# A four-layer attention model on one core: transfers of 29 and 125 rows of layer 2 in two pieces each

## The chip, the core and the metric

The kernel is one program on one core of a Trainium2 chip. The metric is device time in microseconds (us). The profiled core has five compute engines (TensorE, in the views PE, with PEld for its weight loads; VectorE, DVE; ScalarE, ACT; GpSimd, POOL; SyncE, SP, which here only issues transfers) and 16 DMA engines that move data between HBM (DRAM) and the on-chip memories. A DMA goes onto a queue in the order in which SP issues it and counts up a semaphore by 16 when it has landed; whoever needs the data waits for the count.

## What is computed

Four layers of attention and feed-forward run over x (16 batches of 56 tokens, 128 features) with a context of 16 x 1500 x 128. Everything is float32 in layer 2. The change is in layer 2's attention: 16 heads of 64 features, keys and values from the normed context, and one learned null key and value in front.

```python
def _L2_xattn_ref(x, context, mask, ln1_s, ln1_b, lnc_s, lnc_b, Wq, Wkv, null_kv, Wo, lno_s, lno_b):
    ...
    xn = _ln(x, ln1_s, ln1_b)
    cn = _ln(context, lnc_s, lnc_b)
    q = xn @ Wq
    kv = cn @ Wkv
    k, v = jnp.split(kv, 2, axis=-1)
    ...
    k = jnp.concatenate((nk, k), axis=2)
    v = jnp.concatenate((nv, v), axis=2)
    sim = jnp.einsum('bhid,bhjd->bhij', q * scale, k)
    ...
    sim = jnp.where(mfull, sim, max_neg)
    attn = jax.nn.softmax(sim, axis=-1)
    out = jnp.einsum('bhij,bhjd->bhid', attn, v)
    out = out.transpose(0, 2, 1, 3).reshape(b, n, h * d)
    out = out @ Wo
    return _ln(out, lno_s, lno_b)
```

## The kernel before

`attention_16_wide_heads` folds the weights (Wq with Wk, Wv with Wo), so that scores are taken against the normed context itself and the weighted sums are taken of it as well. For each of the 16 batches the 16 heads x 56 queries are 896 rows of queries: seven tiles of 128 (`RT = 7`), 112 tiles in all. The 1500 keys of a batch are laid out as `CH = 125` rows of `NCH = 12` keys each, 128 features (512 bytes) a key, so that one row of the context in DRAM is 6144 bytes. The rows are cut into `WINDOWS = 4` windows: three of `BW = 32` rows, and a last one of `LAST_KEYS = 29` rows. A window gives 12 blocks of 32 keys, and a batch has 48 blocks.

The context goes two ways. For the scores it comes turned (features on partitions, `L2keys`, two slots) and GpSimd norms it there (`normalise_keys`: subtract the means, line 1719, multiply by the scales, line 1721), with means and scales spread over partitions by `load_moments` (L2mean_spread and L2wqk, from L_moments in DRAM). For the weighted sums it comes with keys on partitions: `load_raw` (line 1547) brings 125 rows into L2raw, GpSimd norms them in place (`normalise_values`, lines 1727 and 1729), `store_values` (line 1551) writes the result to DRAM as L_normal_context, and `load_values(b, w)` (line 1560) reads one window of it back four times, into the four quadrants of 32 partitions of L2values. In other words the context is normed once, and the quadrant layout is made by the readback. L2raw is one buffer, so `load_raw(b)` waits until the store before it has landed.

TensorE goes through n = 1, 2, ...: `scores(n)` (line 1636, four matmuls in the program, eight records in the trace) and eight tiles later `weigh(n - 8)` (line 1653), step g of batch b, which takes blocks 7g to 7g + 6 (the last step six) in four quadrants: 56 or 48 records. Step g waits for the windows that its blocks lie in; the sixth step (blocks 35 to 41) is the first to need the last window. Behind `scores`, VectorE takes the maximum (line 1826), ScalarE exponentiates (1764) and scales (1769), VectorE transposes (1836); `take_heads` on ScalarE (1774) empties a batch's sums. ScalarE makes the mask of batch b + 1 (line 1782) between two tiles of batch b, from L2mask, which SP loads.

SP's order is written out by hand: first the fill, down to `load_values(0, w)`, and then for each batch b: keys of b + 1; windows 2 and 3 of b - 1; raw of b + 2; window 0 of b; moments of b + 2; window 1 of b; store of b + 2; mask of b + 2. SP waits before many of these: window w of batch b is loaded when `weigh` is past the last step of batch b - 1 that reads it (`pv_done`), keys when the slot's scores are done, the store when GpSimd has normed (`v_ready`). `TT` is 112.

Of the kernel before, what the change touches and what calls it, by code (L numbers as in the profile page):

```python
# [13 lines left out]
P = 128  # L14
B, Q, S2 = 16, 56, 1500
TOK = B * Q
TT = 2 * Q
NTT = TOK // TT
CH, NCH = 125, 12
# [10 lines left out]
class Vectors:  # L30
# [6 lines left out]
    at = {}  # L37
# [1358 lines left out]
WINDOWS = 4  # L1396
BW = 32
BLOCKS = WINDOWS * NCH
LAST_KEYS = CH - (WINDOWS - 1) * BW
# [3 lines left out]
WORK_COLUMNS = 2 * SM_COLUMNS + CELLS  # L1403
LAG = RT + 1
KEY_COLUMNS = S2 + 3


class WideAhead:
# [61 lines left out]
def attention_16_wide_heads(nc, k, src, ahead):  # L1470
# [8 lines left out]
    with ExitStack() as ctx:  # L1479
# [48 lines left out]
        def block_cells(a, b, block):  # L1528
# [3 lines left out]
                return of.rearrange("p (g r t n) -> p g r t n", g=RT, r=RT, t=RT)[:, g, r]  # L1532
            return of.rearrange("p (t r g n) -> p t r g n", t=RT, r=RT, g=RT)[:, :, r, g]

        def step_blocks(g):
            return range(RT * g, min(RT * g + RT, BLOCKS))

# [2 lines left out]
        @block.sync  # L1540
        def _(sp):
            def load_raw(b):
                if b:
                    sp.wait_ge(s.v_stored, 16 * b)
                else:
                    sp.wait_ge(s.v_zeroed, 2)
                sp.dma_start(RAW[:, :, 0:P - 1], src["ctx"][b][:, :, 0:P - 1]).then_inc(s.raw_loaded, 16)

            def store_values(b):
                sp.wait_ge(s.v_ready, b + 1)  # L1550
                sp.dma_start(normal[b], RAW[:]).then_inc(s.v_stored, 16)

            def load_values(b, w):
                sp.wait_ge(s.v_stored, 16 * (b + 1))
                if b:
                    last_step = (NCH * w + NCH - 1) // RT
                    sp.wait_ge(s.pv_done, RT * (b - 1) + last_step + 1)
                n = BW if w < WINDOWS - 1 else LAST_KEYS
                for a in range(4):
                    sp.dma_start(V[a * BW:a * BW + n, w * NCH:(w + 1) * NCH, :], normal[b][w * BW:w * BW + n]  # L1560
                                 ).then_inc(values_loaded[w], 16)

            def load_mask(b):
                if b:
                    sp.wait_ge(s.mask_ready, 2 * b)
                sp.dma_start(MR[:], src["mask_full"][b].partition_broadcast(P)).then_inc(s.mask_loaded, 16)

            def load_keys(b):
                if b < 2:
                    sp.wait_ge(s.slot_ready, 2 * b + 2)  # L1570
                else:
                    sp.wait_ge(s.scores_filled, RT * (b - 1))
                for rows in (slice(0, TT), slice(TT, P - 1)):
                    sp.dma_start(KT[rows, b % 2, 0:S2], src["ctxT"][b][rows]).then_inc(keys_loaded[b % 2], 16)

            def load_moments(b):
                if b == 1:
                    sp.wait_ge(s.q_filled, 2 * H)
                if b:
                    sp.wait_ge(s.keys_scaled, b)  # L1580
                for x, to in enumerate((MEAN[:], scale_of(b))):
                    sp.dma_start(to, scratch[x, b].rearrange("c n -> (c n)").partition_broadcast(P)).then_inc(s.spread_loaded, 16)

            load_mask(0)
            load_keys(0)
            sp.wait_ge(s.moments_ready, 1)
            sp.dma_start(scratch.rearrange("k (h b) c n -> (b c) (k h) n", h=2), MOMENTS).then_inc(s.moments_stored, 16)
            load_raw(0)
            sp.wait_ge(s.moments_stored, 16)
            load_moments(0)  # L1590
            for a in range(4):
                at = a * BW + LAST_KEYS
                sp.dma_start(V[at:at + 1, BLOCKS - 1, :], k.ident[P - 1:P, :]).then_inc(s.null_rows, 16)
            load_keys(1)
            store_values(0)
            load_raw(1)
            load_moments(1)
            store_values(1)
            load_raw(2)
            load_mask(1)  # L1600
            for w in range(WINDOWS):
                load_values(0, w)
            load_moments(2)
            store_values(2)
            load_mask(2)
            for b in range(1, B + 1):
                ahead_of = b + 2 < B
                if b + 1 < B:
                    load_keys(b + 1)
                if b >= 2:  # L1610
                    load_values(b - 1, 2)
                    load_values(b - 1, 3)
                if ahead_of:
                    load_raw(b + 2)
                if b < B:
                    load_values(b, 0)
                if ahead_of:
                    load_moments(b + 2)
                if b < B:
                    load_values(b, 1)  # L1620
                if ahead_of:
                    store_values(b + 2)
                    load_mask(b + 2)

        @block.tensor
        def _(pe):
# [12 lines left out]
            def weigh(step):  # L1639
                b, g = divmod(step, RT)  # L1640
                if g == 0:
                    pe.wait_ge(s.turned, RT * b + RT)
                    if b:
                        pe.wait_ge(s.heads_ready, 4 * b)
                    else:
                        pe.wait_ge(s.max_done, LAG)
                        pe.wait_ge(s.null_rows, 64)
                blocks = step_blocks(g)
                for w in range(blocks[0] // NCH, blocks[-1] // NCH + 1):
                    pe.wait_ge(values_loaded[w], 64 * (b + 1))  # L1650
                for n in blocks:
                    for a in range(4):
                        last = nc.tensor.matmul(PS[:, 4 + a, 0:RT * BW], V[a * BW:(a + 1) * BW, n, :], block_cells(a, b, n),  # L1653
                                                start=n == 0, stop=n == BLOCKS - 1, tile_position=(a * BW, 0))
                last.then_inc(s.pv_done, 1)
# [55 lines left out]
        @block.gpsimd  # L1711
        def _(pool):
            def normalise_keys(b):
                pool.wait_ge(keys_loaded[b % 2], 32 * (b // 2 + 1))
                pool.wait_ge(s.spread_loaded, 32 * (b + 1))
                if b == 0:
                    pool.wait_ge(s.slot_ready, 4)
                keys = KT[0:P - 1, b % 2, 0:S2]
                nc.gpsimd.tensor_tensor(keys, keys, MEAN[0:P - 1], ALU.subtract).then_inc(s.keys_moved, 1)  # L1719
                pool.wait_ge(s.keys_moved, b + 1)  # L1720
                nc.gpsimd.tensor_tensor(keys, keys, scale_of(b)[0:P - 1], ALU.mult).then_inc(s.keys_scaled, 1)

            def normalise_values(b):
                pool.wait_ge(s.raw_loaded, 16 * (b + 1))
                x = RAW[:, :, 0:P - 1]
                spread = lambda of: of.unsqueeze(2).to_broadcast([CH, NCH, P - 1])
                nc.gpsimd.tensor_tensor(x, x, spread(k.ctx_mv[:, b, :, 0]), ALU.subtract).then_inc(s.v_centred, 1)  # L1727
                pool.wait_ge(s.v_centred, b + 1)
                nc.gpsimd.tensor_tensor(x, x, spread(rs[:, b, :]), ALU.mult).then_inc(s.v_ready, 1)

            for u in range(2):
                nc.gpsimd.memset(KT[:, u, :], 0.0).then_inc(s.slot_ready, 1)
                pool.wait_ge(s.slot_ready, 2 * u + 1)
                nc.gpsimd.tensor_copy(KT[:, u, S2:S2 + 1], k.ident[:, P - 1:P]).then_inc(s.slot_ready, 1)
                if u == 0:
                    ln_pool(pool, k, s)
                    pool.wait_ge(s.ln_rstd, 2)
            nc.gpsimd.memset(RAW[:, :, P - 1:P], 0.0).then_inc(s.v_zeroed, 1)
            nc.gpsimd.memset(V[:, (WINDOWS - 1) * NCH:, :], 0.0).then_inc(s.v_zeroed, 1)
            nc.gpsimd.memset(BIG[:], FLT_MAX).then_inc(s.constants, 1)  # L1740
            for u in range(2):
                nc.gpsimd.memset(MA[:, u, WINDOWS - 1, :, LAST_KEYS:BW], FLT_MAX).then_inc(s.margins, 1)
            for u in range(2):
                pool.wait_ge(s.margins, u + 1)
                nc.gpsimd.memset(MA[:, u, WINDOWS - 1, NCH - 1, LAST_KEYS:LAST_KEYS + 1], 0.0).then_inc(s.margins, 1)
            pool.wait_ge(s.margins, 4)
            normalise_keys(0)
            normalise_values(0)
            normalise_keys(1)
            normalise_values(1)  # L1750
            normalise_values(2)
            for b in range(1, B - 1):
                normalise_keys(b + 1)
                if b + 2 < B:
                    normalise_values(b + 2)
            ln_pool(pool, k, s2)
# [942 lines left out]
```

## Time and profile before

| | us |
|---|---|
| median of 3 runs | 2424.81 |
| lowest, highest | 2419.15, 2427.26 |
| the profiled execution | 2429.18 |
| its span in the trace | 2427.4 |
| layer 2's attention within it, about | 850 to 1880 |
| PE busy over the span | 2000.4 (82%) |
| DVE, ACT, POOL busy | 1416.2, 1256.3, 833.6 |
| granted clock of TensorE, mean | 0.899 |

The profile page gives busy time by engine, by line and in slices; the trace behind it can be asked for one engine's instructions in order of time, for the waits of an engine with what ended them, and for stretches: how long each engine was busy in a stretch, the mean clock that TensorE was granted (1.00 is 2.4 GHz, 0.50 is 1.2 GHz), the mean busy share of the 16 DMA engines and what they moved. A row of SPq is the issue of a transfer, and its time is how long the issue held SP's queue, not how long the transfer took. Merged rows (x8) run from the first start to the last end.

### The profile page before, as it was taken

How to read it: one execution, taken by the hardware profiler on the slowest of the kernel's cores; microseconds unless marked ns; L12 is line 12 of the kernel's file. 1: busy time of each engine (PE TensorE's matmuls, PEld its weight loads, DVE VectorE, ACT ScalarE, POOL GpSimd, SP SyncE). 2: the span in 40 equal slices, each digit the busy share in tenths (PEclk: the TensorE clock that was granted, in tenths of full speed). 3: DMA queues.
4: the chain of work that ended last, by engine and by line, in shares of the span. 5: the costliest groups of instructions: out<-in, count | busy, mean ns of one | idle time of the engine just before them, and what ended most of it. 6: DMA issues, size and time to landing. Idle time of an engine off the chain costs nothing. (4 is left out here: it accounts for less than half of the span.)

```text
span 2427.4 us, 51483 instructions
## 1 busy us (share of the span) xinstructions
PE 2000.4 (82%) x21121; PEld 1419.8 (58%) x21121; DVE 1416.2 (58%) x2762; ACT 1256.3 (52%) x2169; POOL 833.6 (34%) x376
## 2 busy tenths in 40 slices
PE   6999999669988993877776666666687779999997
PEld 3777777458874462555554444444465436777774
DVE  5777777789855443544444444444440667777784
ACT  5787877337652233544444444444440247777773
POOL 6656562157756532221212121212100044444410
PEclk8999999679998986988888888888888889999997
DMA  6454542325403043544344444344420144444430
GB/s 164 137 152 137 150 139 78 87 72 142 141 18 80 26 120 107 135 119 119 120 121 120 122 121 119 119 119 119 132 69 11 31 120 139 138 130 137 134 93 9
DMA packets 130282, 263.70 MB, mean 109 GB/s; under 512 B 69456, under 2 KB 77696, under 8 KB 129792
## 3 DMA queue, kind: packets, MB, share of 16 engines
q1 hardware_dynamic: 130048, 260.40, 37.6%
q8 instruction: 168, 2.75, 0.5%
q14 instruction: 66, 0.54, 0.1%
HBM read 167.57 MB, written 12.94 MB: 74 GB/s over the span
## 5 line engine op out<-in xcount | busy, mean ns | idle before, releaser
L1653 PE MATMUL L2ps<-L2work,L2values 32*128 32x224 f32 x6144 | 354.9, 382 | 241.4 <-DMA L2values<-L_normal_context 235.6
L1653 PEld LDWEIGHTS L2ps<-L2work,L2values 32*128 32x128 f32 x6144 | 318.1, 203 | 302.0 <-issue 295.2
L1836 DVE STREAM_TRANSPOSE L2work<-L2work 128x1568 f32<-128x1568 f32 x112 | 202.9, 1811 | 369.3 <-PE L2ps L1653 367.7
L1769 ACT ACTIVATE L2work<-L2work,L2rinv 128x1536 f32<-128x1536 f32 x112 | 176.8, 1579 | 370.9 <-DVE L2rinv L1841 370.9
L1636 PE MATMUL L2ps<-L2keys,L2qz 128*128 128x384 f32 x896 | 329.7, 510 | 42.5 <-DVE L2negmax L1826 35.1
L1826 DVE CUSTOM_DVE_ANT_0 L2work<-L2ps,L2maskadd,L2big 128x1536 f32<-128x1536 f32 x112 | 203.6, 1818 | 105.0 <-PE L2ps L1636 105.0
L1636 PEld LDWEIGHTS L2ps<-L2keys,L2qz 128*128 128x128 f32 x896 | 161.8, 190 | 173.9 <-issue 39.9
L1764 ACT ACTIVATE L2work<-L2work,L2negmax 128x1536 f32<-128x1536 f32 x112 | 176.2, 1573 | 119.9 <-DVE L2negmax L1826 119.8
L654 ACT ACTIVATE L3probsT<-L3ps 128x448 f32<-128x448 f32 x384 | 196.1, 547 | 71.0 <-PE L3ps L511 66.4
L654 ACT ACTIVATE L0probsT<-L0ps 128x448 f32<-128x448 f32 x384 | 198.2, 552 | 47.5 <-PE L0ps L511 46.4
L798 DVE TENSOR_REDUCE L0partmax<-L0ps 112x1 f32<-112x1000 f32 x128 | 153.4, 1199 | 58.7 <-PE L0ps L484 56.8
L1727 POOL TENSOR_TENSOR L2raw<-L2raw,ctx_mv 125x1524 f32<-125x1524 f32 x16 | 43.9, 2743 | 417.8 <-DMA L2raw<-in_ctx 417.8
L798 DVE TENSOR_REDUCE L3partmax<-L3ps 112x1 f32<-112x1000 f32 x128 | 153.4, 1198 | 57.6 <-PE L3ps L484 55.4
L511 PEld LDWEIGHTS L0ps<-L0query_stack,L0key_stack 99*128 99x128 bf16 x1536 | 110.6, 99 | 57.4 <-issue 13.6
L1719 POOL TENSOR_TENSOR L2keys<-L2keys,L2mean_spread 127x1500 f32<-127x1500 f32 x16 | 49.8, 3110 | 270.9 <-DMA L2keys<-in_ctxT 230.2
L511 PEld LDWEIGHTS L3ps<-L3query_stack,L3key_stack 98*128 98x128 bf16 x1536 | 110.5, 99 | 54.8 <-issue 13.8
L511 PE MATMUL L0ps<-L0query_stack,L0key_stack 99*128 99x112 bf16 x1536 | 134.0, 214 | 0.7 <-ACT L0probsT L654 0.6
L511 PE MATMUL L3ps<-L3query_stack,L3key_stack 98*128 98x112 bf16 x1536 | 133.3, 214 | 0.0
L605 POOL TENSOR_TENSOR L3keys<-L3keys,L3key_parts 128x1500 f32<-128x1500 f32 x16 | 48.6, 3037 | 193.3 <-ACT L3key_parts L701 193.3
L793 DVE TENSOR_REDUCE L0partmax<-L0ps 112x1 f32<-112x500 f32 x128 | 86.3, 674 | 33.1 <-PE L0ps L476 33.1
L793 DVE TENSOR_REDUCE L3partmax<-L3ps 112x1 f32<-112x500 f32 x128 | 86.2, 673 | 30.8 <-PE L3ps L476 30.8
L498 PE MATMUL L3ps<-L3probsT,L3values 128*32 128x112 f32 x3072 | 99.8, 263 | 0.0
(478 smaller groups left out, 3877.1 us busy)
## 6 DMA issues: line engine op xcount, KB each, us to landing
L2values<-L_normal_context SPq DMA_DIRECT2D x192, 192.0 KB
L0key_stack<-L0key_parts SPq DMA_DIRECT2D x192, 187.5 KB
L3key_stack<-L3key_parts SPq DMA_DIRECT2D x192, 187.5 KB
L0ctxT<-in_ctxT SPq DMA_DIRECT2D x16, 750.0 KB, 4.4
L1rawT<-in_ctxT SPq DMA_DIRECT2D x16, 750.0 KB, 6.5
L2mean_spread<-L_moments SPq DMA_DIRECT2D x16, 750.0 KB, 7.2
L_normal_context<-L2raw SPq DMA_DIRECT2D x16, 750.0 KB
L3ctxT<-in_ctxT SPq DMA_DIRECT2D x16, 750.0 KB, 4.4
```

Of the source, the lines that this page charges most:

```text
L498: last = nc.tensor.matmul(PS[32 * g:32 * g + 32, 3, u * TT:(u + 1) * TT], V[:, b % 2, value_columns(c, 4 * u + g)], PT[:, u, c, g, :], sta ...
L511: last = nc.tensor.matmul(PS[:, bank, c * TT:(c + 1) * TT], KS[:, h % 4, tau, key_columns(4 * j + c)], QS[:, h % 4, tau, :], start=True, s ...
L654: ins = nc.scalar.activation(PT[:, h % 2, 4 * j:4 * j + 4, tau, :], PS[:, bank, 0:HALF].rearrange("p (c n) -> p c n", c=4), ACT.Exp)
L793: nc.vector.tensor_reduce(PM[:, h % 2, tau, 0:1], PS[0:TT, 0, 0:500], AX.X, ALU.max).then_inc(s.m0_done, 1)
L798: nc.vector.tensor_reduce(PM[:, h % 2, tau, 1:2], PS[0:TT, 1:3, 0:500], AX.XY, ALU.max).then_inc(s.m12_done, 1)
L1636: last = nc.tensor.matmul(PS[:, score_bank(m) + w, 0:NCH * BW], tile_rows(m), key_window(b, w), start=True, stop=True)
L1653: last = nc.tensor.matmul(PS[:, 4 + a, 0:RT * BW], V[a * BW:(a + 1) * BW, n, :], block_cells(a, b, n), start=n == 0, stop=n == BLOCKS - 1, ...
L1719: nc.gpsimd.tensor_tensor(keys, keys, MEAN[0:P - 1], ALU.subtract).then_inc(s.keys_moved, 1)
L1764: nc.scalar.activation(SM[:, m % 2, 0:NPR], SM[:, m % 2, 0:NPR], ACT.Exp, bias=nmax[:, m % 4:m % 4 + 1], scale=-1.0, accum_out=ssum[:, m % ...
L1769: nc.scalar.mul(SM[:, m % 2, 0:NPR], SM[:, m % 2, 0:NPR], rinv[:, m % 4:m % 4 + 1]).then_inc(s.scaled, 1)
L1826: nc.vector.tensor_tensor_reduce(SM[:, m % 2, 0:NPR].rearrange("p (w n) -> p w n", w=WINDOWS), PS[:, bank:bank + 4, 0:NCH * BW], MA[:, m / ...
L1836: nc.vector.transpose(turned_cells(b, t), SM[:, m % 2].rearrange("p (g r n) -> p g r n", g=RT, n=BW)).then_inc(s.turned, 1)
```

## The change

`load_raw` and `store_values` send their 125 rows as two transfers, of 112 and of 13 rows. `load_values` sends the last window's 29 rows, for each of the four quadrants, as 16 and 13 rows; the other windows stay transfers of 32 rows. The same bytes go to the same places. The counts that are waited for follow: 32 for each batch of raw and of the store in place of 16, and 128 in place of 64 for the last window.

```diff
--- before.py
+++ after.py
@@ -1403,6 +1403,7 @@
 WORK_COLUMNS = 2 * SM_COLUMNS + CELLS
 LAG = RT + 1
 KEY_COLUMNS = S2 + 3
+WHOLE, SHORT = (slice(0, BW),), (slice(0, BW // 2), slice(BW // 2, LAST_KEYS))
 
 
 class WideAhead:
@@ -1532,6 +1533,9 @@
                 return of.rearrange("p (g r t n) -> p g r t n", g=RT, r=RT, t=RT)[:, g, r]
             return of.rearrange("p (t r g n) -> p t r g n", t=RT, r=RT, g=RT)[:, :, r, g]
 
+        window_rows = lambda w: WHOLE if w < WINDOWS - 1 else SHORT
+        values_count = lambda b, w: 64 * len(window_rows(w)) * (b + 1)
+
         def step_blocks(g):
             return range(RT * g, min(RT * g + RT, BLOCKS))
 
@@ -1541,24 +1545,26 @@
         def _(sp):
             def load_raw(b):
                 if b:
-                    sp.wait_ge(s.v_stored, 16 * b)
+                    sp.wait_ge(s.v_stored, 32 * b)
                 else:
                     sp.wait_ge(s.v_zeroed, 2)
-                sp.dma_start(RAW[:, :, 0:P - 1], src["ctx"][b][:, :, 0:P - 1]).then_inc(s.raw_loaded, 16)
+                for rows in (slice(0, TT), slice(TT, CH)):
+                    sp.dma_start(RAW[rows, :, 0:P - 1], src["ctx"][b][rows, :, 0:P - 1]).then_inc(s.raw_loaded, 16)
 
             def store_values(b):
                 sp.wait_ge(s.v_ready, b + 1)
-                sp.dma_start(normal[b], RAW[:]).then_inc(s.v_stored, 16)
+                for rows in (slice(0, TT), slice(TT, CH)):
+                    sp.dma_start(normal[b][rows], RAW[rows]).then_inc(s.v_stored, 16)
 
             def load_values(b, w):
-                sp.wait_ge(s.v_stored, 16 * (b + 1))
+                sp.wait_ge(s.v_stored, 32 * (b + 1))
                 if b:
                     last_step = (NCH * w + NCH - 1) // RT
                     sp.wait_ge(s.pv_done, RT * (b - 1) + last_step + 1)
-                n = BW if w < WINDOWS - 1 else LAST_KEYS
                 for a in range(4):
-                    sp.dma_start(V[a * BW:a * BW + n, w * NCH:(w + 1) * NCH, :], normal[b][w * BW:w * BW + n]
-                                 ).then_inc(values_loaded[w], 16)
+                    for rows in window_rows(w):
+                        to, of = (slice(at + rows.start, at + rows.stop) for at in (a * BW, w * BW))
+                        sp.dma_start(V[to, w * NCH:(w + 1) * NCH, :], normal[b][of]).then_inc(values_loaded[w], 16)
 
             def load_mask(b):
                 if b:
@@ -1647,7 +1653,7 @@
                         pe.wait_ge(s.null_rows, 64)
                 blocks = step_blocks(g)
                 for w in range(blocks[0] // NCH, blocks[-1] // NCH + 1):
-                    pe.wait_ge(values_loaded[w], 64 * (b + 1))
+                    pe.wait_ge(values_loaded[w], values_count(b, w))
                 for n in blocks:
                     for a in range(4):
                         last = nc.tensor.matmul(PS[:, 4 + a, 0:RT * BW], V[a * BW:(a + 1) * BW, n, :], block_cells(a, b, n),
@@ -1721,7 +1727,7 @@
                 nc.gpsimd.tensor_tensor(keys, keys, scale_of(b)[0:P - 1], ALU.mult).then_inc(s.keys_scaled, 1)
 
             def normalise_values(b):
-                pool.wait_ge(s.raw_loaded, 16 * (b + 1))
+                pool.wait_ge(s.raw_loaded, 32 * (b + 1))
                 x = RAW[:, :, 0:P - 1]
                 spread = lambda of: of.unsqueeze(2).to_broadcast([CH, NCH, P - 1])
                 nc.gpsimd.tensor_tensor(x, x, spread(k.ctx_mv[:, b, :, 0]), ALU.subtract).then_inc(s.v_centred, 1)
```

Nothing else changes its place; line numbers below line 1406 grow by 1 to 6. SP's part for one batch in the middle of the stage, before:

```order
L1574 DMA L2keys<-in_ctxT 112x1500
L1574 DMA L2keys<-in_ctxT 15x1500
L1560 DMA L2values<-L_normal_context 32x1536 x4
L1560 DMA L2values<-L_normal_context 29x1536 x4
L1547 DMA L2raw<-in_ctx 125x12x127
L1560 DMA L2values<-L_normal_context 32x1536 x4
L1582 DMA L2mean_spread<-L_moments 128x1500
L1582 DMA L2wqk<-L_moments 128x1500
L1560 DMA L2values<-L_normal_context 32x1536 x4
L1551 DMA L_normal_context<-L2raw 125x1536
L1566 DMA L2mask<-in_mask_full 128x1500
```

And the same place in the changed kernel. L2wqk holds the scales from L_moments here; of the last window's eight transfers the first two stand:

```order
L1580 DMA L2keys<-in_ctxT 112x1500
L1580 DMA L2keys<-in_ctxT 15x1500
L1567 DMA L2values<-L_normal_context 32x1536 x4
L1567 DMA L2values<-L_normal_context 16x1536
L1567 DMA L2values<-L_normal_context 13x1536
```

Three more pairs of 16 and 13 rows follow, and then:

```order
L1552 DMA L2raw<-in_ctx 112x12x127
L1552 DMA L2raw<-in_ctx 13x12x127
L1567 DMA L2values<-L_normal_context 32x1536 x4
L1588 DMA L2mean_spread<-L_moments 128x1500
L1588 DMA L2wqk<-L_moments 128x1500
L1567 DMA L2values<-L_normal_context 32x1536 x4
L1557 DMA L_normal_context<-L2raw 112x1536
L1557 DMA L_normal_context<-L2raw 13x1536
```

SP's order is kept: the keys, the two windows, raw, window 0, moments, window 1, store, and 23 transfers of a batch become 29. The second place is the fill, on SP too: the stores of batches 0 and 1, the loads of raw 1 and 2, and the mask of batch 1. Before:

```order
L1551 DMA L_normal_context<-L2raw 125x1536
L1547 DMA L2raw<-in_ctx 125x12x127
L1582 DMA L2mean_spread<-L_moments 128x1500
L1582 DMA L2wqk<-L_moments 128x1500
L1551 DMA L_normal_context<-L2raw 125x1536
L1547 DMA L2raw<-in_ctx 125x12x127
L1566 DMA L2mask<-in_mask_full 128x1500
```

In the changed kernel:

```order
L1557 DMA L_normal_context<-L2raw 112x1536
L1557 DMA L_normal_context<-L2raw 13x1536
L1552 DMA L2raw<-in_ctx 112x12x127
L1552 DMA L2raw<-in_ctx 13x12x127
L1588 DMA L2mean_spread<-L_moments 128x1500
L1588 DMA L2wqk<-L_moments 128x1500
L1557 DMA L_normal_context<-L2raw 112x1536
L1557 DMA L_normal_context<-L2raw 13x1536
L1552 DMA L2raw<-in_ctx 112x12x127
L1552 DMA L2raw<-in_ctx 13x12x127
L1572 DMA L2mask<-in_mask_full 128x1500
```

Store, raw and the mask of batch 1 stay in this order, with a transfer of 13 rows behind each of 112.

## Rows read from the trace of the kernel before

**Rows 1.** Waits of PE, 960 to 1860: total us, times, longest us.

```profile
PE L2ps L1653 <- DMA L2values<-L_normal_context: 235.6, 28, 18.6
PE L2ps L1636 <- POOL L2keys L1721: 7.2, 1, 7.2
```

**Rows 2.** PE in order of time: start, us, line, operation, tiles, count, idle time before.

```profile
1209.99 2.93 PE L1653 MATMUL L2ps<-L2work,L2values 32*128 32x224 f32 x56
...
1231.51 4.67 PE L1653 MATMUL L2ps<-L2work,L2values 32*128 32x224 f32 x56 [15.75 <-DMA L2values<-L_normal_context]
...
1238.97 2.55 PE L1653 MATMUL L2ps<-L2work,L2values 32*128 32x224 f32 x48
...
1250.99 2.93 PE L1653 MATMUL L2ps<-L2work,L2values 32*128 32x224 f32 x56 [0.91 <-DMA L2values<-L_normal_context]
...
1290.29 4.30 PE L1653 MATMUL L2ps<-L2work,L2values 32*128 32x224 f32 x56 [16.39 <-DMA L2values<-L_normal_context]
...
1526.37 5.61 PE L1653 MATMUL L2ps<-L2work,L2values 32*128 32x224 f32 x56 [16.17 <-DMA L2values<-L_normal_context]
```

**Rows 3.** Stretches: window, length, PE, PEld, DVE, ACT, POOL busy, PEclk, DMA share, GB/s.

```profile
1172.00:1231.00 59.00, 41.59 (x440) 29.67 (x440) 25.78 (x28) 25.11 (x27) 12.22 (x4) 0.85 0.40 121
1194.00:1212.00 18.00, 18.00 (x218) 12.92 (x214) 11.05 (x12) 9.48 (x10) 6.74 (x2) 1.00 0.27 85
1222.00:1230.00 8.00, 0.00 (x0) 0.00 (x0) 0.00 (x0) 0.00 (x0) 0.00 (x0) 0.50 0.06 26
1212.00:1221.00 9.00, 3.77 (x28) 2.00 (x22) 3.68 (x4) 6.40 (x7) 0.00 (x0) 0.84 0.31 93
1240.00:1247.00 7.00, 7.00 (x98) 5.18 (x92) 4.68 (x6) 4.85 (x8) 5.48 (x2) 1.00 1.00 309
546.50:551.00 4.50, 4.29 (x29) 3.20 (x28) 3.97 (x27) 4.44 (x13) 3.37 (x3) 1.00 0.90 224
```

**Rows 4.** SP's queue in order of time, 1246 to 1306, its longest entries.

```profile
1250.58 12.75 SPq L1560 DMA_DIRECT2D L2values<-L_normal_context  x8
1263.37 7.20 SPq L1547 DMA_DIRECT2D L2raw<-in_ctx  x1
...
1270.68 25.41 SPq L1560 DMA_DIRECT2D L2values<-L_normal_context  x4
...
1297.13 2.39 SPq L1560 DMA_DIRECT2D L2values<-L_normal_context  x4
```

**Rows 5.** PE in order of time: the wait for keys, and the last steps.

```profile
1001.37 5.32 PE L1636 MATMUL L2ps<-L2keys,L2qz 128*128 128x384 f32 x8 [7.21 <-POOL L2keys L1721]
...
1807.50 6.88 PE L1653 MATMUL L2ps<-L2work,L2values 32*128 32x224 f32 x104 [2.29 <-DMA L2values<-L_normal_context]
...
1844.50 7.64 PE L1653 MATMUL L2ps<-L2work,L2values 32*128 32x224 f32 x104 [11.68 <-DMA L2values<-L_normal_context]
```

**Rows 6.** The fill, 862 to 949, all engines in order of time.

```profile
862.58 26.23 PE L1682 MATMUL L2ps<-xnT,L2wqk 128*128 128x448 f32 x64 [0.84 <-DVE xnT L163]
...
911.64 2.85 POOL L1719 TENSOR_TENSOR L2keys<-L2keys,L2mean_spread 127x1500 f32<-127x1500 f32 x1 [23.37 <-DMA L2wqk<-L_moments]
...
922.94 0.28 SPq L1551 DMA_DIRECT2D L_normal_context<-L2raw  x1
930.42 0.82 SPq L1547 DMA_DIRECT2D L2raw<-in_ctx  x1
931.29 6.08 SPq L1566 DMA_DIRECT2D L2mask<-in_mask_full  x1
...
942.88 1.26 ACT L1782 ACTIVATE L2maskadd<-L2mask,L2big 128x1152 f32<-128x1152 uint8 x1 [31.04 <-DMA L2mask<-in_mask_full]
...
948.22 10.29 PE L1636 MATMUL L2ps<-L2keys,L2qz 128*128 128x384 f32 x24 [33.21 <-DVE L2negmax L1826]
```

**Rows 7.** The page's part on DMA issues: count, KB each, median us to landing.

```profile
L0ctxT<-in_ctxT SPq DMA_DIRECT2D x16, 750.0 KB, 4.4
...
L2mean_spread<-L_moments SPq DMA_DIRECT2D x16, 750.0 KB, 7.2
```

## What the change should do, before it was run

> **What bounds the kernel now.** I read the waits of PE in the stretch of layer 2's attention first, then PE's order in time over two batches, then what the DMA engines did while PE stood still, then SP's order in time. The first view says where the time is: of the 900 us that it covers, PE stood 235.6 us for L2values, in 28 waits, and 7.2 us for keys [rows 1]. The second shows the pattern: one long wait a batch (13.4 to 18.6 us, 13 of them), always before the sixth of the seven steps of `weigh`, the first that needs the last window (29 rows), and a wait under 1 us at the second step [rows 2]. After each long wait the next step takes 4.30 to 5.61 us where an undisturbed one takes 2.93 [rows 2]: the granted clock is 0.50 while PE stands and 1.00 while it works [rows 3], so that is the lower of the two levels, 1.2 against 2.4 GHz. Between waits PE is busy 18.00 of 18.00 us, with VectorE at 11.05, ScalarE at 9.48 and GpSimd at 6.74 [rows 3]: nothing but the transfers stands in PE's way.
>
> The third view says why the transfers are late. While PE waits, DMA share is 0.06 and 26 GB/s: one engine of 16 [rows 3]. The four transfers of 29 rows are 4 x 174 KB = 0.71 MB, and 0.71 MB at 26 GB/s is 27.4 us. With the 125-row load of L2raw issued behind them the share is 0.31 [rows 3], five of 16: four with the load's parts, the fifth still with the 29 rows. So I read that 29 rows go through one engine and 125 rows through five, of which that one is a member. Its time in one batch is then: 29-row transfers 27.4; its fifth of L2raw 9 (the others take 1212 to 1221); its fifth of the 125-row store, 154 KB at 26 GB/s, 5.9; and a sixteenth of the rest. A batch moves 59 us x 121 GB/s = 7.1 MB [rows 3]; less 0.71, 0.76 and 0.77 that leaves 4.9 MB, which at 309 GB/s, all engines busy [rows 3], takes 15.9 us. Sum 58.2 us, against a batch of 1290.29 - 1231.51 = 58.8 us [rows 2]. The bound is one DMA engine, not PE. SP shows the same: four of its entries hold the queue 12.75 + 7.20 + 25.41 + 2.39 = 47.8 us a batch, though the same kind of four transfers takes 2.39 once and 25.41 another time [rows 4].
>
> **The change part by part.** (1) Each 29-row transfer becomes 16 + 13 rows, each 125-row one 112 + 13. Bytes stay. The trace has no 13-row transfer by itself; the nearest stretch is layer 1's attention, which loads its context as 112 + 13 rows, where the share is 0.90 at 224 GB/s, mixed with other loads [rows 3]. Best end: all spreads, 7.1 MB at 309 GB/s is 23 us of engine time a batch. Worst end: every 13-row piece stays on one engine. Then that one has 52 of 116 rows of the last window (12.3 us), 13 rows of raw (13/125 x 5 x 9 = 4.7), 13 of the store (80 KB, 3.1), its sixteenth of the 112- and 16-row pieces (1.4 MB at 309 GB/s, 4.5) and the 15.9 of before: 40.5 us. I take the spread end, by the 0.90 of layer 1, and keep the other for the range.
>
> The Trainium skill, DMA: Bandwidth & Descriptors, "Why a DMA increments its semaphore by 16 and not by 1", says that a transfer issued from SP uses the largest number up to 16 that divides its row count: 1 for 29, 5 for 125, 16 for 112 and for 16, 13 for 13. The trace agrees for 29 and 125 (shares 0.06 and 0.31), and shows neither 13 nor 16 alone. By that rule the sum is that of the spread end.
>
> (2) What PE needs for a batch when it never waits: 58.8 - 16.39 - 0.91 - (4.67 - 2.93) = 39.8 us [rows 2]. The 23 us of transfers fit, and they have time to land: the last window's are released at the end of step seven of the batch before and needed before step six, five and a half of seven steps or 31 us on; their eight issues cost some 0.5 us each (2.39 for four [rows 4]) and 0.71 MB at 309 GB/s is 2.3 us, under 10 us with what lies in front. So all of the 235.6 us goes, and what is late next is nothing: max, exp, scale and turn kept up with PE at exactly this rate in the 18 us above. Term: 235.6.
>
> (3) PE's slow step after each of the 13 long waits, 4.30 to 5.61 (lowest and highest shown, mean of the 13 5.00) [rows 2], goes too: 13 x (5.00 - 2.93) = 26.9.
>
> (4) One wait for keys, 7.2 us [rows 1], with eight records of `scores` in 5.32 behind it [rows 5], where 2.9 is the undisturbed figure: those keys were loaded late by the same held queue. Term: 9.6.
>
> (5) The end: two groups of 104 take 6.88 and 7.64 [rows 5] where 2.93 + 2.55 less overlap is 5.4 [rows 2]. Term: 3.7.
>
> (6) The fill. PE stands 33.21 us before 948.22; the chain behind it is mask(1), which ScalarE awaits 31.04 us, until 942.88 [rows 6]. Back from it: mask(1) is issued behind raw(2) and held 6.08; raw(2) waits 7.5 us for store(1) to land; store(1) follows GpSimd's keys(1) and values(1), 11.3 us from 911.64; and keys(1) waited for moments(1) [rows 6]. Afterwards: moments(1) can go out at 888.8, when PE's 26.23 us group ends; with 0.3 us for issue and a landing of 7.2 [rows 7] keys(1) starts at about 896.5; store(1) 907.8; landing 4.4, the row of a 750 KB transfer without a queue [rows 7], raw(2) at 912.2; mask(1) lands 12.5 - 6.1 = 6.4 later, about 919. That is 24 us sooner. The bounds: 31.0, when mask(1) is never awaited, and 10 if raw and store gain nothing but the 6.08 and half of the store's 7.5. The 3 MB of values for batch 0 go out from 913 and need 10 us, before the first `weigh` at about 937. Term: 24.
>
> (7) Added: per batch four issues for values, one for raw, one for the store, 6 x 0.5 = 3 us of SP. SP then has some 13 us of work in 39.8, so it costs nothing; if SP were still held all the time it would be 16 x 3 = 48. The counts waited for grow with the number of transfers, so nobody waits for less or more data. SP's waits for `pv_done` and `v_ready` still stand in front of the transfers queued behind them, each over 20 us ahead of its reader.
>
> Sum: 235.6 + 26.9 + 9.6 + 3.7 + 24 = 299.8. Against the profiled execution, 2429.2 (span 2427.4 and 1.8 around it), that is 2129.4. This execution lies 4.4 above the median 2424.8, so for the median I forecast **2125**.
>
> **Rivals.** (A) The 13-row pieces do not spread. One engine has 40.5 us a batch against PE's 39.8, so short waits stay, 1 to 2 us with a slow step behind some: 15 x 2.5 = 38, 2163. For it: no row shows such a piece alone. Against: 0.90 in layer 1.
> (B) The change doesn't do what it says: two pieces take together what one took, and one engine keeps them. The batch stays at 58.8 and the time at 2425. Against it: the share of 0.06 leaves 15 engines with nothing to do. The Trainium skill, DMA: Bandwidth & Descriptors, "Rules for kernel authors", says just this: don't split a transfer into disjoint partition halves, they serialize on the same 16 engines. It supposes that the whole used all 16; the row with 0.06 says otherwise here.
> (C) Slower: SP's hold is a price of each transfer and not of a full engine behind it. Four entries hold SP 47.8 us for 17 transfers, 2.8 each; six more add 17 us, and 47.8 + 17 = 64.8 exceeds the 58.8 of a batch by 6: 2425 + 15 x 6 = 2515. It decides from 11/6 = 1.8 us for each added transfer. Against it: four of the same take 2.39 us together [rows 4].
> (D) The fill gains only 10, or a wait of about 1 us a batch remains at the second step: 14 to 15 more, 2140. That is within the forecast's own spread.
>
> **How the numbers follow.** Forecast with (D), 2112 to 2145: 0.80. (A), 2145 to 2175: 0.11. (B), 2405 to 2435: 0.04. (C): 0.03. The rest, 0.02, is another bound between 2175 and 2400. The low end is the sum with 31 in the fill and 5 more for the last steps and the clock; the high end takes in (A) up to 2168. This range holds about 0.9, since the price of (A) is no clearer than this. A measurement of this kernel can tell about 0.3%, 7 us, from no change: faster 0.94, same 0.03, slower 0.03.
>
> **What would show it.** In the profile of the changed kernel: no PE wait of more than 3 us for L2values; batches 39.8 us apart; the DMA share never at 0.06 for more than 3 us inside this stage, and about 175 GB/s on average; SP's entries for raw under 2 us; the clock at 1.00 over the stage; mask(1) landed near 919. Wrong would be: a share of 0.06 behind the 13-row pieces (A), unchanged waits (B), SP entries of over 1.8 us for each small piece (C).

## The result, and the profile after it

The changed kernel takes 2123.72 us (median of 4 runs, 2121.64 to 2124.81) against 2426.03 us of the kernel before: the ratio is 0.8754, 95% interval 0.8729 to 0.8778. The forecast was 2125, with a range of 2112 to 2168. Run again it took 2123.34 us, ratio 0.8761 (0.8749 to 0.8773).

The waits of TensorE from 900 to 1570 in the changed kernel (total us, times, longest), which answer to [rows 1]:

```profile
PE L2ps L1642 <- DVE L2negmax L1832: 12.3, 5, 10.0
PE L2ps L1659 <- DVE L2work L1842: 5.8, 2, 3.2
PE L2ps L1712 <- ACT L2qz L1780: 1.2, 1, 1.2
```

The 28 waits for L2values and the one for keys are gone. What is left lies in the fill (12.3) and at the two ends of the batches' chain (5.8). In the middle of the stage, TensorE in order of time, answering to [rows 2]:

```profile
1131.36 2.55 PE L1659 MATMUL L2ps<-L2work,L2values 32*128 32x224 f32 x48
...
1170.94 2.55 PE L1659 MATMUL L2ps<-L2work,L2values 32*128 32x224 f32 x48
```

These are the last steps of two batches in a row, 39.58 us apart. In the kernel before, the forecast took 58.8 from one pair of batches; the last steps from 1006.62 to 1474.53 are 58.5 apart in the mean of eight. The stretch from 1000 to 1450, with the columns of [rows 3] (window, length, busy times, granted clock, DMA share, GB/s):

```profile
1000.00:1450.00 450.00, 450.00 (x5017) 315.11 (x5019) 293.27 (x320) 285.83 (x307) 129.12 (x44) 1.00 0.72 180
```

TensorE is busy 450.00 of 450.00 us at a clock of 1.00, the DMA engines are busy 0.72 of the time instead of 0.40, and the same bytes go at 180 GB/s instead of 121. SP's queue over one batch, answering to [rows 4]:

```profile
1137.27 1.68 SPq L1552 DMA_DIRECT2D L2raw<-in_ctx  x2
1145.44 2.39 SPq L1567 DMA_DIRECT2D L2values<-L_normal_context  x4
...
1156.88 2.52 SPq L1567 DMA_DIRECT2D L2values<-L_normal_context  x4
...
1170.10 6.71 SPq L1567 DMA_DIRECT2D L2values<-L_normal_context  x12
```

Two transfers of raw hold SP 1.68 us where one held it 7.20, and window 0 takes 2.39 where it took 25.41. The fill, answering to [rows 6], and the end of the stage, answering to [rows 5]:

```profile
919.08 1.26 ACT L1788 ACTIVATE L2maskadd<-L2mask,L2big 128x1152 f32<-128x1152 uint8 x1 [7.79 <-DMA L2mask<-in_mask_full]
...
924.41 6.97 PE L1642 MATMUL L2ps<-L2keys,L2qz 128*128 128x384 f32 x16 [9.96 <-DVE L2negmax L1832]
...
937.24 4.62 PE L1659 MATMUL L2ps<-L2work,L2values 32*128 32x224 f32 x56 [2.54 <-DVE L2work L1842]
...
1529.65 18.44 PE L1659 MATMUL L2ps<-L2work,L2values 32*128 32x224 f32 x384 [3.23 <-DVE L2work L1842]
```

The mask of batch 1 lands at 919.08 (before 942.88), TensorE resumes at 924.41 (before 948.22), and the last sums end at 1548.09 (1529.65 + 18.44) where they ended at 1852.14 (1844.50 + 7.64): 304.0 us of the 304.4 by which the spans differ.

### The profile page after: what moved, and what is told of

Same layout as the page of the kernel before. It is cut to its first block and busy times, and to the rows that moved or that the text cites. A ratio compares the mean times of both kernels' runs of the same rounds, so it can differ in the third digit from the quotient of the medians.

```text
span 2123.0 us, 51579 instructions
## 1 busy us (share of the span) xinstructions
PE 1962.9 (92%) x21121; PEld 1386.9 (65%) x21121; DVE 1415.5 (67%) x2762; ACT 1255.4 (59%) x2169; POOL 833.1 (39%) x376
## 5 line engine op out<-in xcount | busy, mean ns | idle before, releaser
L1642 PE MATMUL L2ps<-L2keys,L2qz 128*128 128x384 f32 x896 | 327.0, 507 | 12.3 <-DVE L2negmax L1832 12.3
L1659 PEld LDWEIGHTS L2ps<-L2work,L2values 32*128 32x128 f32 x6144 | 285.4, 186 | 64.5 <-issue 57.8
L1659 PE MATMUL L2ps<-L2work,L2values 32*128 32x224 f32 x6144 | 321.9, 356 | 5.8 <-DVE L2work L1842 5.8
L511 PEld LDWEIGHTS L0ps<-L0query_stack,L0key_stack 99*128 99x128 bf16 x1536 | 110.6, 99 | 58.5 <-issue 13.5
L498 PE MATMUL L3ps<-L3probsT,L3values 128*32 128x112 f32 x3072 | 99.8, 263 | 0.0
L498 PE MATMUL L0ps<-L0probsT,L0values 128*32 128x112 f32 x3072 | 99.7, 263 | 0.0
```

Source lines behind the costliest of these rows:

```text
L498: last = nc.tensor.matmul(PS[32 * g:32 * g + 32, 3, u * TT:(u + 1) * TT], V[:, b % 2, value_columns(c, 4 * u + g)], PT[:, u, c, g, :], sta ...
L511: last = nc.tensor.matmul(PS[:, bank, c * TT:(c + 1) * TT], KS[:, h % 4, tau, key_columns(4 * j + c)], QS[:, h % 4, tau, :], start=True, s ...
L1642: last = nc.tensor.matmul(PS[:, score_bank(m) + w, 0:NCH * BW], tile_rows(m), key_window(b, w), start=True, stop=True)
```

## The experiments

The forecast rested on one sum: how long one DMA engine is busy with a batch, against how long TensorE is. The experiments take the change apart, and then vary the row count alone, with the number of transfers kept.

**Only the last window in two pieces.** Raw and store are whole again.

```diff
-                for rows in (slice(0, TT), slice(TT, CH)):
+                for rows in (slice(0, CH),):
                     sp.dma_start(RAW[rows, :, 0:P - 1], ...
...
-                for rows in (slice(0, TT), slice(TT, CH)):
+                for rows in (slice(0, CH),):
                     sp.dma_start(normal[b][rows], RAW[rows]) ...
```

The counts that are waited for are 16 a batch again too.

> Only the last window's 29 rows go as 16 + 13; raw and store are 125 rows in one transfer again. Theory (one DMA engine's time per batch sets the batch before, PE's 39.8 us after): that engine has 9 (its fifth of raw) + 5.9 (store) + about 1 (last window) + 15.9 (its sixteenth of the rest) = 32 us, under 39.8, so PE never waits for values in the middle and batches stay 39.5 to 39.8 us apart; only the fill loses its 24 us: 2124 + 24 = 2148 (2140 to 2160). Rival (raw, the widest transfer in descriptors, is what held SP 7 to 25 us a batch): with raw whole SP stays held and most of the waits come back, over 2250.

Measured: 2145.68 us, ratio 0.8856 (0.8834 to 0.8878), which is 22.0 more than the changed kernel. TensorE's waits over the stage, and its restart in the fill:

```profile
PE L2ps L1642 <- DVE L2negmax L1832: 30.9, 1, 30.9
PE L2ps L1659 <- DVE L2work L1842: 5.1, 2, 3.2
```

```profile
945.26 11.02 PE L1642 MATMUL L2ps<-L2keys,L2qz 128*128 128x384 f32 x24 [30.92 <-DVE L2negmax L1832]
```

No wait for values is left, which rules out the rival, the batches are 39.5 to 39.6 us apart, and the whole loss is the fill: TensorE restarts at 945.26 and not at 924.41, 20.9 us later, and the spans of the two traces differ by 20.9 (2143.9 and 2123.0). So, with 16 + 13 rows in the last window, its split makes the middle and that of raw and store the fill.

**Only raw and store in two pieces.** The last window is one transfer of 29 rows.

```diff
-WHOLE, SHORT = (slice(0, BW),), (slice(0, BW // 2), slice(BW // 2, LAST_KEYS))
+WHOLE, SHORT = (slice(0, BW),), (slice(0, LAST_KEYS),)
```

> Only raw and store are split into 112 + 13; the last window is 29 rows in one transfer, four times. Theory: one engine has 27.4 (29 rows, 0.71 MB at 26 GB/s) + 6.4 MB over all engines at 309 GB/s = 20.7, together 48.1 us a batch: PE waits about 8 us before the sixth step, batches 48 us apart, 2124 + 15 x 8.3 = 2248 (2220 to 2275), the fill as in the changed kernel (mask of batch 1 at about 919). Rival (raw held SP): about 2124 to 2140, without long waits.

Measured: 2307.26 us, ratio 0.9525 (0.9505 to 0.9546), some 59 us slower than expected and outside the range. Its SP queue and one stretch in which nothing else was left to move:

```profile
1197.25 24.46 SPq L1552 DMA_DIRECT2D L2raw<-in_ctx  x2
```

```profile
1152.00:1168.00 16.00, 12.28 (x131) 8.20 (x129) 9.23 (x11) 11.02 (x10) 0.00 (x0) 0.98 0.07 27
```

For 16 us the DMA share is 0.07 at 27 GB/s, one engine of 16, and the two issues of raw, 112 and 13 rows here, hold SP for 24.46 us in the next batch (23.03 in this one). The mechanism is the forecast's (raw did not hold SP by itself: the rival's 2124 to 2140 is out), but the batches are 51.4 to 53.6 us apart, not 48.

**The same number of transfers, other row counts: 23 + 6, 28 + 1, 12 + 17.** All else as in the changed kernel.

```diff
-WHOLE, SHORT = (slice(0, BW),), (slice(0, BW // 2), slice(BW // 2, LAST_KEYS))
+WHOLE, SHORT = (slice(0, BW),), (slice(0, 23), slice(23, LAST_KEYS))
```

and in its place `(slice(0, 28), slice(28, LAST_KEYS))` and `(slice(0, 12), slice(12, LAST_KEYS))`.

> As the changed kernel, but the last window goes as 23 + 6 rows: the same number of transfers and bytes, another row count. Theory (a row count without a divisor up to 16 sits on one engine): 4 x 23 rows = 0.565 MB at 26 GB/s = 21.7 us, and 6.5 MB over all engines = 21.1, and under 1 for the 6 rows: 43.5 us a batch against 39.8, so 2124 + 15 x 3.7 = 2180 (2150 to 2205), waits of 3 to 5 us before the sixth step. Rival (what helps is the smaller transfer, or two in flight at once): 2124 to 2130 as the changed kernel.

> As the changed kernel, but the last window goes as 28 + 1 rows. Theory (28 rows spread over 14 engines, and four single rows cost one engine 1 us): 2124 (2118 to 2130), no waits for values. Rival (only row counts that are a multiple of 16 spread, 13 rows too few to matter): 28 rows on one engine, 26.5 + 20.7 = 47 us a batch, 2124 + 15 x 7.4 = 2235.

> As the changed kernel, but the last window goes as 12 + 17 rows. Theory: 17 rows sit on one engine, 4 x 17 rows = 0.418 MB at 26 GB/s = 16.1 us, with 6.7 MB over all engines 21.6: 37.7 us a batch, just under PE's 39.8. So 2124 (2118 to 2140) although a transfer without a divisor is there: it costs only when its engine's sum passes PE's. Rival (any transfer on one engine is late for its reader, whatever the sum): waits of some us a batch, 2170 and more.

Measured: 23 + 6 takes 2240.2 us (ratio 0.9246, 0.922 to 0.9271), 28 + 1 takes 2123.1 (0.8767, 0.8749 to 0.8785), 12 + 17 takes 2176.8 (0.8966, 0.895 to 0.8982). One stretch of the kernel with 23 rows:

```profile
1188.00:1196.00 8.00, 8.00 (x75) 5.36 (x72) 5.54 (x6) 4.21 (x6) 0.00 (x0) 1.00 0.07 28
```

and one of that with 17:

```profile
1202.00:1211.00 9.00, 9.00 (x105) 6.32 (x108) 6.10 (x7) 4.82 (x4) 0.00 (x0) 1.00 0.06 27
```

Both leave one engine at work, as 29 rows did; 28 rows leave no stretch of 6 us or more like it, and no wait. A smaller transfer, or two in flight, is then not what helped: 23 + 6 and 16 + 13 differ by 116 us with the same count and bytes. Nor does a count have to be a multiple of 16: 28 + 1 equals the change. By the rule of the Trainium skill (DMA: Bandwidth & Descriptors, "Why a DMA increments its semaphore by 16 and not by 1"), that the largest divisor up to 16 sets the number of engines, 23 and 17 get one and 28 gets 14. The shares of 0.07 and 0.06 agree with it for 23 and 17; for 28 the absence of waits shows that it is not one engine, and not that it is 14.

But 23 + 6 was expected at 2180 and 12 + 17 at 2124, so here too the size was wrong, by 60 and 53 us, as by 59 in the run before. Three misses of one sign and size pointed to the term that all three share.

**The term that failed.** In all three the part of a batch that is spread over 16 engines had been taken at 309 GB/s, 23 us. The changed kernel shows it directly, as the mean of its 16 engines: a share of 0.73 over 40 us is 29.2 us. (The long stretch, 0.72 over a batch of 39.6, gives 28.5; the sums below use 29.2, as the forecasts of the next runs do, and would be 0.4 to 0.7 us lower with 28.5.) With 29.2 for 7.1 MB the sums are 53.7, 48.6 and 43.6 us, and the batches were 52.1, 47.5 and 43.4 apart (means between 1000 and 1450). Three more kernels were made to test this sum where it forecasts something of its own.

**Half of the quadrants: 12 + 17, or 29 whole.** Quadrants 0 and 1 differ, 2 and 3 keep 16 + 13.

```diff
-        window_rows = lambda w: WHOLE if w < WINDOWS - 1 else SHORT
+        window_rows = lambda w, a=0: WHOLE if w < WINDOWS - 1 else OTHER if a < 2 else SHORT
...
-                    for rows in window_rows(w):
+                    for rows in window_rows(w, a):
```

with `OTHER` as 12 + 17 rows in the first, and as 29 rows (and the count waited for to match) in the second.

> As the changed kernel, but two of the four quadrants take the last window as 12 + 17 rows, the other two as 16 + 13. Theory, mended after e2, e3 and e5 (the part that all 16 engines share takes each of them 29.2 us a batch, share 0.73 of 40 us in the changed kernel, not 23): 2 x 17 rows = 0.209 MB at 26 GB/s = 8.0 us on one engine, and 29.2 x 6.9/7.1 = 28.3: 36.4 us against 39.6, so no waits and 2124 (2119 to 2131). Rival (each transfer on one engine costs its reader some us, whatever the sum): half of what e5 lost, 53/2: 2150.

> As the changed kernel, but two of the four quadrants take the last window as 29 rows in one transfer. Mended theory: 2 x 29 rows = 0.356 MB = 13.7 us and 29.2 x 6.75/7.1 = 27.7: 41.4 us against 39.6, 15 x 1.8 = 27: 2151 (2135 to 2165). The first theory (23 us shared): 13.7 + 21.8 = 35.5, no waits, 2124. Rival (by whole transfers): half of what e2 lost, 183/2: 2215.

Measured: 2123.76 us for the first (ratio 0.8761, 0.8745 to 0.8777), without waits and with batches 39.5 to 39.6 apart; 2136.99 for the second (0.8819, 0.8805 to 0.8833), with these waits of TensorE:

```profile
PE L2ps L1660 <- DMA L2values<-L_normal_context: 13.6, 9, 2.4
```

So the same 17-row transfers on one engine, which cost 53 us when all four quadrants used them, cost nothing when two do: it is the sum that decides, not the single transfer. The second lies in its range near the lower end, with batches of 39.5 to 43.2 us where 41.4 was worked out.

**Raw and store whole again, with 12 + 17.**

> The last window as 12 + 17 rows, raw and store whole in 125 rows as in the kernel before. Mended theory: the same engine has 16.1 (17 rows), 9 + 5.9 (its fifths of raw and store) and 29.2 x 5.2/7.1 = 21.4: 52 us, and since this way of counting came out 1 to 4 us high in e2 and e3, batches of 49 to 52 us; with the 22 us that e1 lost in the fill: 2124 + 22 + 15 x (9.5 to 12.5) = 2289 to 2334. Rival (raw and store cost nothing in the middle, as e1 seems to say): 2177 + 22 = 2199.

The edit is that of the first experiment with that of 12 + 17. Measured: 2284.83 us, ratio 0.9426 (0.9409 to 0.9443); the waits:

```profile
PE L2ps L1659 <- DMA L2values<-L_normal_context: 104.9, 35, 8.3
```

That is 4 us below the range given and 86 above the rival. The batches are 49.9 us apart, within the 49 to 52 given. Part of why the time still came out lower is the factor of 15: the last batch has no scores beside its sums (18.44 us in the changed kernel), so 14 full periods are paid, and 2146 + 14 x 10.3 is 2290. The 5 us that remain are open. Whole transfers of 125 rows cost 22 us beside 16 + 13, all in the fill, but 108 beside 12 + 17 (2284.8 - 2176.8), where each batch grows by 6.5 us (49.9 - 43.4) and the sum by 8.6. Their share on that engine is free as long as its sum stays under TensorE's 39.6 us, and the greater part of it is paid above.

All kernels in one table, with the mended sum (the engine's own transfers at 26 GB/s, raw's fifth 9 us and the store's 5.9 where whole, and the spread part at 29.2 us for 7.1 MB):

| last window | raw, store | sum for one engine, us | batch measured, us | median, us |
|---|---|---|---|---|
| 29 | whole (before) | 62.5 | 58.5 | 2424.8 |
| 29 | split | 53.7 | 52.1 | 2307.3 |
| 12 + 17 | whole | 52.2 | 49.9 | 2284.8 |
| 23 + 6 | split | 48.6 | 47.5 | 2240.2 |
| 12 + 17 | split | 43.6 | 43.4 | 2176.8 |
| 29 in two quadrants | split | 41.4 | 40.8 | 2137.0 |
| 16 + 13 | whole | 37.8 | 39.6 | 2145.7 |
| 12 + 17 in two quadrants | split | 36.4 | 39.6 | 2123.8 |
| 16 + 13 (the change) | split | 29.2 | 39.6 | 2123.7 |

Below 39.6 TensorE sets the batch, above it the one engine. The sum is a little high where that engine's own part is large, 4.0 us in the kernel before. I did not test why; the spread part was measured with all engines sharing it closely, and it may go faster where they have more room. The stretches bear this out in part only. In the kernel before the share is 0.41 from 1231 to 1290, which is 387 us of all 16 engines together; less 27.4 and five times 14.9 (raw and store) that leaves 17.8 each for the spread part, where the sum took 20.2. With 12 + 17 rows and split raw and store the same working (0.68 over 43.4 us, less 16.1) leaves 28.5, where it took 27.5. From row to row the order is as the sum says; its size holds to 2.3 us or better, and to 4.0 in the kernel before.

**The mask of batch 1 earlier.** The changed kernel's fill still has ScalarE waiting 7.79 us for this mask and TensorE 9.96 behind it.

```diff
+            load_mask(1)
             store_values(1)
             load_raw(2)
-            load_mask(1)
```

> As the changed kernel, but in the fill the mask of batch 1 is loaded ahead of the store of batch 1 and raw of batch 2. Theory: in the changed kernel ScalarE still awaits this mask 7.8 us and PE stands 10.0 us behind it; the mask then lands before 905 and both waits go; the first weighing starts 8 us sooner if the values of batch 0, sent from 913, are there by 929: 2124 - 8 = 2116 (2113 to 2120). Rival: the values of batch 0 are what comes last then, and a wait for them takes up to all of the 8: 2119 to 2124.

Measured: 2115.7 us, ratio 0.8717 (0.8698 to 0.8736). The fill:

```profile
909.88 2.92 PE L1642 MATMUL L2ps<-L2keys,L2qz 128*128 128x384 f32 x8 [2.07 <-DVE L2negmax L1832]
...
922.71 4.62 PE L1659 MATMUL L2ps<-L2work,L2values 32*128 32x224 f32 x56 [2.54 <-DVE L2work L1842]
```

The wait of 9.96 us is 2.07 now, about the time that ScalarE needs to make the mask, and the values are there in time. Since part of the difference in this trace lay ahead of the stage, both kernels were run again on one chip:

> The changed kernel once more, on the same chip as the next run, so that the two can be compared directly: 2124 (2119 to 2128).

> The kernel with the mask of batch 1 loaded early once more. Theory: 8 us less than the changed kernel on the same chip, 2116 (2112 to 2120). Rival: the 8 us between e6 and the changed kernel came from another chip and from a stretch ahead of this stage; then both are equal within 3 us.

2123.34 against 2117.17 us; the ratios to the kernel before are 0.8761 (0.8749 to 0.8773) and 0.8731 (0.8717 to 0.8745), just apart. The gain is 6.2 us, somewhat less than the 8 of theory and 0.3% of the time, near the least that such runs can tell; this is the fastest kernel of the study. The traces show that the gain is not one number. In the second trace of the changed kernel TensorE had worked off the group of 64 matmuls ahead of the scores by 880.75 and not by 888.26, stands 16.15 us for the mask in place of 9.96, and starts the first `weigh` at 935.93, 1.3 us sooner: there the mask hides what an earlier stretch gained or lost. With the mask out of the way it shows: 922.71 and 926.89 for the first `weigh` in the two traces, and times from 2109.48 to 2121.27, where the changed kernel has 2120.41 to 2125.14.

## Why the forecast came out right, and where it was luck

- **What bounds the kernel before.** Right. One DMA engine of 16 was the bound; the row counts 29, 23 and 17 each put a transfer on one.
- **The sum of that engine.** Wrong in one term. The spread part of a batch was taken from a 7 us stretch at 309 GB/s; over a batch it goes at 243 GB/s in the time that the engines are busy (7.1 MB in 29.2 us). No single rate holds at full share: two single microseconds of the changed kernel, both near 1.00, moved 426 and 166 GB/s, the second just as window 1 and the two pieces of the store were issued.

```profile
1271.00:1272.00 1.00, 1.00 (x4) 0.56 (x3) 0.70 (x2) 0.26 (x1) 0.00 (x0) 1.00 1.02 426
1278.00:1279.00 1.00, 1.00 (x17) 0.83 (x20) 0.71 (x1) 1.00 (x1) 0.00 (x0) 1.00 0.93 166
```

The agreement of 58.2 with the batch of 58.8 was partly luck: with the mended term the sum is 62.5, 4 us high. The forecast for the change did not hang on it, since both 23 and 29.2 are under TensorE's time. Every forecast near the threshold did: three experiments missed by 53 to 60 us.
- **TensorE's own 39.8 us.** Right: 39.5 to 39.6. VectorE, ScalarE and GpSimd kept up over 450 us as they had over the 18 that the forecast pointed to.
- **The spread of 13 rows.** Taken at the spread end from the mixed stretch of layer 1. Right, and the changed kernel's trace shows it for the store. The store of batch 0 is issued at 881.10 with all DMA engines at rest, and this is the stretch in which its 112 and its 13 rows move:

```profile
881.75:884.75 3.00, 3.00 (x10) 1.52 (x9) 1.25 (x2) 1.08 (x3) 0.00 (x0) 1.00 0.80 256
```

256 GB/s times 3.00 us is the whole 0.77 MB. If the 13 rows were on one engine, it would need 3.1 us for them and 1.7 for its seven of the 112 rows, at 26 GB/s, and the share could not be 0.80. SP's next issue, raw of batch 1, waits for both pieces and comes 4.2 us after the store's; before it came 7.7 after (888.30 and 895.97).
- **Waits for values, 235.6, and for keys, 7.2.** Right, both are gone. One reading behind them was loose and changed nothing: the wait at the second step was called under 1 us, and in the trace it is 0.36 to 3.03, over 1 in 7 of 13 batches.
- **The slow steps and the clock.** Right: the clock is 1.00 over the stretch of 450 us and no step is slow in it. From the first `weigh` to the end of the last one (961.05 to 1852.14, now 937.24 to 1548.09) the stage shrank by 280.2; the terms for it (235.6 + 26.9 + 9.6 + 3.7) make 275.8. Of the 4.4 us that are missing, up to 2.7 are slow matmuls that the terms left out: TensorE's busy time for scores and sums fell from 329.7 + 354.9 to 327.0 + 321.9, 35.7 us, and the terms hold 33.0 of it. The rest stayed unassigned.
- **The fill.** Right: the first `weigh` starts 23.8 us earlier, the sum said 24, and the mask (919) and the first `weigh` (937) came within 0.3 us of the times given. The steps between did too, within 1.2 us: moments(1) out at 888.29, keys(1) at 895.53, store(1) at 906.84, raw(2) at 911.04. Putting raw and store back cost 22.0. A little luck is in the first step: moments(1) was to go out when TensorE's group of 64 ends, and in the second trace of this kernel that is 880.75, but moments(1) goes out at 886.54, right behind raw(1), which had waited for the store. In the first trace the two conditions are 1.4 us apart (886.84 and 888.26), so the sum did not feel it.
- **SP's six more issues a batch.** Free, as said: SP is not held.
- **The rival of 13 rows on one engine.** Not borne out, but its price of 2163 was too low. The 16- and 112-row pieces are 1.76 MB (0.39 + 0.68 + 0.69), not 1.4. By the mended sum that engine has 12.3 + 4.7 + 3.1 of its own, 7.3 of these pieces and 20.2 of the rest, 47.6 us a batch, and that is about 2240. The range to 2168 did not cover that rival as it claimed to.

## What to carry to other kernels

Before asking how many bytes a transfer has, look at the DMA share while the reader waits: 0.06 of 16 engines at 26 to 28 GB/s over many microseconds means that one of them has the work, and another row count (28 + 1, 16 + 13) can be worth more than any reordering. (A short stretch can mislead: the changed kernel has 0.06 and 23 GB/s from 1282 to 1288, but there all engines are at rest from 1283 to 1287 and busy at either end.) Sum up what the busiest engine does in one period and compare it with the compute engine's time; below that a badly spread transfer is free, above it most of it is paid in each period (here the batch grew by 15.1 us from 43.4 to 58.5 while the sum grew by 18.9). Take the rate of the shared part from a stretch as long as the period, since a short one at its peak flatters it, and treat a sum that fits only one measured case as unproven.

## What was not expected

- The spread part of a batch, 7.1 MB of rows of 6 KB and pieces of 508 bytes, keeps 16 engines busy 28.5 to 29.2 us, 243 to 250 GB/s of busy time, though a stretch at share 1.00 moved 309 GB/s [rows 3].
- A spread transfer queued behind one on a single engine holds SP as long as that engine is behind: 24.46 us for raw's two pieces with 29 rows in front, against 1.68 in the changed kernel. In these traces SP's hold follows the fullest engine, not the transfer being issued: raw whole, in five parts, holds SP 0.79 us where the last window is 16 + 13 (1156.46 in the first experiment). No view shows the queue itself, so that is read from the holds alone.
